# Moving the subtraction and clamp of five of eight decay tiles into the slots of the conv units, in place in the broadcast tiles

## What is computed

```
A_cum  = cumsum(dt * A)                       # per head, over a chunk
L      = exp(A_cum[l] - A_cum[s])  for l >= s, else 0
Y_diag = einsum('bzlhn,bzshn,bhzls,bzshp->bzlhp', Cc, Bc, L, xch)
...
xc     = silu(depthwise_conv(hBC))            # 4 taps over the tokens
g      = y * silu(gate);  out = normed(g) @ out_proj_w.T
```

## Time and profile before

| | |
|---|---|
| time, median of 3 runs | 2678.79 us (2675.01 to 2682.47) |
| the profiled execution | 2688.24 us, its span 2686.5 us |
| granted TensorE clock, mean | 0.980 |
| busy over the span | TensorE 93%, VectorE 69%, ScalarE 58%, GpSimd 53% |
| the mixer | from 1066.4 us to 2573.9 us of the span |

### The profile page before, as it was taken

How to read it: one execution, slowest core, us unless ns; L and a number is a source line. 1 busy time by engine, 2 the same in 40 slices (tenths; PEclk the granted TensorE clock), 3 DMA queues, 4 the chain that set the end, 5 groups by cost and what they waited for, 6 DMA issues and landing times.

```text
span 2686.5 us, 60496 instructions
## 1 busy us (share of the span) xinstructions
PE 2508.8 (93%) x19326; PEld 2014.3 (75%) x19326; DVE 1859.6 (69%) x2707; ACT 1565.2 (58%) x3539; POOL 1425.6 (53%) x1396
## 2 busy tenths in 40 slices
PE   5999999999999678899999999999999999999989
PEld 4778788788788467677777777777777777777777
DVE  4776666766767677677777677687677777786864
ACT  3544535535445254766865775786677658757821
POOL 1654655656546000556656565575666566565720
PEclk8999999999999789999999999999999999999999
DMA  4022220220230024323222222222232132222111
GB/s 111 26 81 42 50 78 29 65 74 23 75 70 8 19 91 145 109 64 108 95 67 89 96 84 68 96 100 68 80 107 85 64 104 99 76 78 94 56 40 48
DMA packets 93549, 198.84 MB, mean 74 GB/s; under 512 B 11248, under 2 KB 19440, under 8 KB 93296
## 3 DMA queue, kind: packets, MB, share of 16 engines
q1 hardware_dynamic: 93296, 195.64, 23.3%
HBM read 184.46 MB, written 11.14 MB: 73 GB/s over the span
## 4 chain that ended last, share of the span: by engine, by line
PE 28%; DVE 12%; issue 10%; ACT 10%; POOL 5%; ACTq 1%; DVEq 1%; DMA 0%; POOLq 0%; SPq 0%
PE proj L214 6%; PE proj L216 6%; PE proj L215 6%; DVE mx_acc L1170 3%; ACT decay L1484 3%; ACT mx_decay L1484 2%; PE core_y L1360 2%; DVE slab_lo L197 2%; POOL mx_hd L1629 1%; POOL mx_gate L1633 1%; ACT mx_HS L1470 1%; PE core_o L1366 1%; DVE bc_acc L1170 1%; ACT mx_decay L1488 1%; DVE mx_hd L1547 1%
## 5 line engine op out<-in xcount | busy, mean ns | idle before, releaser
L197 DVE TENSOR_TENSOR slab_lo<-slab_raw,slab_hi 128x512 fp32r<-128x512 f32 (+2 forms) x272 | 262.8, 978 | 177.2 <-ACT slab_hi L188 149.7
L214 PE MATMUL proj<-slab_hi,XTL 128*128 128x512 f32 x816 | 348.6, 427 | 5.1 <-DVE mx_gate L1576 2.7
L214 PE MATMUL proj<-XTH,slab_lo 128*128 128x512 f32 x736 | 301.2, 409 | 35.0 <-DVE at_ropeB L874 14.1
L216 PE MATMUL proj<-slab_hi,XTH 128*128 128x512 f32 x816 | 320.1, 392 | 0.0
L215 PE MATMUL proj<-slab_lo,XTH 128*128 128x512 f32 x816 | 319.0, 391 | 0.0
L215 PE MATMUL proj<-XTL,slab_hi 128*128 128x512 f32 x736 | 292.5, 397 | 0.0
L216 PE MATMUL proj<-XTH,slab_hi 128*128 128x512 f32 x736 | 292.4, 397 | 0.0
L1616 POOL TENSOR_TENSOR mx_th<-mx_th,mx_acc 128x512 f32<-128x512 f32 x48 | 62.2, 1296 | 370.3 <-ACT mx_th L1515 370.3
L214 PE MATMUL proj<-slab_hi,mx_otl 128*128 128x512 f32 x576 | 241.7, 420 | 2.1 <-DVE mx_otl L263 2.1
L1633 POOL TENSOR_TENSOR mx_gate<-mx_gate,mx_hd 128x512 f32<-128x512 f32 x128 | 170.2, 1330 | 133.1 <-DVE mx_hd L1547 122.1
L216 PE MATMUL proj<-slab_hi,mx_oth 128*128 128x512 f32 x576 | 227.6, 395 | 0.0
(11 more groups left out here) (353 smaller groups left out, 6770.0 us busy)
## 6 DMA issues: line engine op xcount, KB each, us to landing
mx_g_all<-sums SPq DMA_DIRECT2D x128, 512.0 KB, 3.7
at_g_all<-sums SPq DMA_DIRECT2D x64, 256.0 KB, 8.0
slab_raw<-in_w_gate SPq DMA_DIRECT2D x64, 256.0 KB, 2.9
slab_raw<-in_w_out SPq DMA_DIRECT2D x64, 256.0 KB, 2.9
slab_raw<-in_w_x SPq DMA_DIRECT2D x60, 256.0 KB, 4.4
slab_raw<-in_w_q SPq DMA_DIRECT2D x32, 256.0 KB, 2.9
slab_raw<-in_w_g SPq DMA_DIRECT2D x32, 256.0 KB, 8.4
slab_raw<-in_w_o SPq DMA_DIRECT2D x32, 256.0 KB, 2.9
```

Source lines behind the costliest of these rows:

```text
L197: op = nc.vector.tensor_tensor(K.SL[par][:, c, 0:width], K.RAW[c][:, 0:width], hi, ALU.subtract)
L214: nc.tensor.matmul(to[:, 0:bh.shape[-1]], al, bh, start=(c == 0), stop=False)
L216: mm = nc.tensor.matmul(to[:, 0:bh.shape[-1]], ah, bh, start=False, stop=(c == KC - 1))
```

## The change

The Relu of a tile is written back into its `GB` tile instead of into the bank, and the Exp reads from there. So the Relu no longer needs the bank, and those of tiles 1 to 4 are put behind the tanh in the conv slots 0 to 7 (one half tile, four Relu, per slot), those of tile 0 into slots 21 and 22 of the half before. Tiles 5 to 7 keep their slots, but both half tiles' Relu now stand ahead of both Exp. A fifth `GB` tile is added; tiles 0 to 2 share theirs with 5 to 7, and the row loads wait for other readers. A plain `nop` (`alone`) is issued ahead of each row load. No instruction that computes is added or removed.

```diff
-        GB = [sb(f"g_all{i}", [P, HH1, P]) for i in range(4)]
+        GB = [sb(f"g_all{i}", [P, HH1, P]) for i in range(5)]
+        ROW_OF = [0, 1, 2, 3, 4, 0, 1, 2]
+        EARLY = {sl: (sl // 2 + 1, sl % 2) for sl in range(8)}
+        NEXT = {OFF + 13: (0, 0), OFF + 14: (0, 1)}
...
-            def row_load(q, t):
-                sp.wait_ge(S["mx_e"], HEAD + 16 * q + 2 * t - 6)
+            def row_load(q, t, read):
+                i = ROW_OF[t]
+                src = sums[t:t + 1, ds(HH1 * P * q, HH1 * P)].broadcast_to([P, HH1 * P])
+                sp.wait_ge(S["mx_e"], HEAD + 16 * q + read)
+                alone(sp)
...
-            for t in range(4):
-                row_load(0, t)
+            for t in range(5):
+                row_load(0, t, 0)
...
-                    for t in range(4, NT):
-                        row_load(q, t)
+                    for t in range(5, NT):
+                        row_load(q, t, 2 * (t - 5) + 2)
...
-                        for t in range(4):
-                            row_load(q + 1, t)
+                        for t, reader in ((3, 3), (4, 4), (0, 5), (1, 6), (2, 7)):
+                            row_load(q + 1, t, 2 * reader + 2 - 16)
...
+            def differences(q, t, k):
+                i = ROW_OF[t]
+                act.wait_ge(S[f"mx_row{i}"], HEAD + (32 * q + 16 * (1 + (t >= 5)) if i < 3 else 16 * (q + 1)))
+                alone(act)
+                for h in range(4 * k, 4 * k + 4):
+                    rl = nc.scalar.activation(GB[i][:, h, :], GB[i][:, h, :], ACT.Relu,
+                                              bias=upto[:, t, ds(HH1 * q + h, 1)], scale=-1.0)
+                rl.then_inc(S["mx_rl"], 1)
...
                     if r in SCORE1:
                         t = SCORE1.index(r)
-                        act.wait_ge(S[f"mx_row{t % 4}"], HEAD + 32 * q + 16 * (t // 4 + 1))
+                        if t >= 5:
+                            for k in range(2):
+                                differences(q, t, k)
                         for k in range(2):
                             act.wait_ge(S["mx_m"], HEAD + 16 * q + 2 * t + k - 1)
...
-                            alone(act)
-                            for h in range(4):
-                                rl = nc.scalar.activation(PD[k][:, h * P:(h + 1) * P], GB[t % 4][:, 4 * k + h, :], ACT.Relu,
-                                                          bias=upto[:, t, ds(HH1 * q + 4 * k + h, 1)], scale=-1.0)
-                            rl.then_inc(S["mx_rl"], 1)
                             act.wait_ge(S["mx_rl"], HEAD + 16 * q + 2 * t + k + 1)
-                            nc.scalar.activation(PD[k][:, :], PD[k][:, :], ACT.Exp, scale=-1.0).then_inc(S["mx_e"], 1)
+                            nc.scalar.activation(PD[k][:, :], GB[ROW_OF[t]][:, 4 * k:4 * k + 4, :].rearrange("p h n -> p (h n)"), ACT.Exp,
+                                                 scale=-1.0).then_inc(S["mx_e"], 1)
...
+                    if sl in EARLY:
+                        differences(q, *EARLY[sl])
+                    if sl in NEXT and not (last and s == 1):
+                        differences(q + 1, *NEXT[sl])
+            for k in range(2):
+                differences(0, 0, k)
```

More of the change, by code:

```diff
@@ L165 @@
     + ["bc_ld", "bc_a", "bc_tap", "bc_cm", "bc_st0", "bc_st1", "bc_st2", "bc_st3"]
-    + ["mx_ld", "mx_bc", "mx_row0", "mx_row1", "mx_row2", "mx_row3", "mx_a", "mx_tap", "mx_th", "mx_cm", "mx_hsT", "mx_pt", "mx_hs",
+    + ["mx_ld", "mx_bc", "mx_row0", "mx_row1", "mx_row2", "mx_row3", "mx_row4", "mx_a", "mx_tap", "mx_th", "mx_cm", "mx_hsT", "mx_pt", "mx_hs",
        "mx_pof", "mx_cb", "mx_bt", "mx_e", "mx_m", "mx_xc", "mx_hd", "mx_xd", "mx_y", "mx_yb",
@@ L1310, in slab @@
                     load_chunk(K, sp, N + 3 * q + j, c, whole(w[ds(q + (j == 3), 1), :, c, :]))
-            def row_load(q, t):
-                sp.wait_ge(S["mx_e"], HEAD + 16 * q + 2 * t - 6)
-                sp.dma_start(GB[t % 4][:, :, :].rearrange("p h n -> p (h n)"), sums[t:t + 1, ds(HH1 * P * q, HH1 * P)]
-                             .broadcast_to([P, HH1 * P])).then_inc(S[f"mx_row{t % 4}"], 16)
+            def row_load(q, t, read):
[3 more added lines that the diff above has]
+                alone(sp)
+                sp.dma_start(GB[i][:, :, :].rearrange("p h n -> p (h n)"), src).then_inc(S[f"mx_row{i}"], 16)
             sp.dma_start(tri[:, :], d["tri"]).then_inc(S["mx_ld"], 16)
```

## The result

The changed kernel takes 2652.11 us (median of 4 runs, 2650.94 to 2656.66); the kernel before, on the same chip, 2680.63 (4 runs, 2675.01 to 2687.98). The ratio is 0.9895 with a 95% interval of 0.9867 to 0.9923: 28.5 us less (21 to 36), where 15.5 were forecast (2663.3, range 2650 to 2680). The profiled execution took 2650.94, its span 2649.2.

A forecast was written before the change was run, and what follows sets the result against it. TensorE bounds the kernel, finally waiting for ScalarE's overfull queue in slots 8 to 14. Terms -13.0 - 5.0 + 0.7 + 1.8 = -15.5 us, from a median of 2678.79 to 2663.3, range 2650 to 2680.

The forecast's parts named there:

- Step 1: Relu out of slots 8 to 14: waits for gated tile, `HS` copies and slot 10 gate go, 29.6 us gross.
- Step 2: Relu into even halves' conv slots: no cost to TensorE, each half keeps a 1.62 us gain, 13.0 for eight.
- Step 3: Relu into odd halves' conv slots: 0.3 late at slot 7, 1.0 at slot 10; net -0.62 per half, -5.0 us.
- Step 4: Tiles 5 to 7, both groups ahead of both Exp: late waits (`mx_xch`, `mx_hd`) stay, zero effect.
- Step 5: Tile 0's Relu in slots 21 and 22: delays the last tile's high part in even halves, 0.7 us lost.
- Step 6: SyncE's fifth row load ahead of the first weights: 1.8 us lost once at the start; other loads no later.
- ScalarE becomes the bound of the conv slots: Rival, 10%: at 1.5 instead of 1.18 us per group, conv slots delay each silu; +10 us, 2689.
- The gain is eaten by the next in line: Rival, 17%: VectorE or GpSimd holds the gated tile, slot 14's wait only halves; -4 us in total, 2675.
- The conv slots hide everything: Rival, 15%: ScalarE's waits for TensorE in most conv slots absorb the moved Relu; 2651 to 2655 us.

## Why the forecast had the direction and the mechanism right and the size too small

*Step 1* (the Relu out of slots 8 to 14) held. All three waits are gone, and with them the 29.6 us that they cost by the forecast's count. It was a little more: from the turn in slot 12 to that in slot 14 an even half went from 9.4 to 8.1 us, 1.3 and not the 1.13 that I had counted.

*Step 2* (even halves at no cost) held: no new wait, the middle is 1.9 shorter, against 1.62 forecast. In sum that is 15 for 13.0. A whole even half between two turns of the loop takes 91.2 to 92.4 us in both profiles, under the 92.6 forecast.

*Step 3* (odd halves) had the chain right and its result too small. Its links, ScalarE and GpSimd in conv slots 4 and 7 of an odd half and TensorE at slots 7 and 10, of the changed kernel:

```profile
1546.76 0.77 ACT L1160 ACTIVATE mx_acc<-mx_decay,conv_b,conv_w 128x512 f32<-128x512 f32 x1
1547.42 0.62 ACT L1527 ACTIVATE mx_to<-mx_hd 128x512 f32<-128x512 f32 x1
1547.94 1.28 ACT L1457 ACTIVATE mx_g_all<-mx_g_all,upto_sum 128x128 f32<-128x128 f32 x4
...
1555.99 0.78 ACT L1160 ACTIVATE mx_hd<-core_y,conv_b,conv_w 128x512 f32<-128x512 f32 x1
```

```profile
1548.19 1.30 POOL L1634 TENSOR_TENSOR mx_to<-mx_to,mx_hd 128x512 f32<-128x512 f32 x1 [0.63 <-ACT mx_to L1527]
1549.64 1.30 POOL L1637 TENSOR_TENSOR mx_hd<-mx_to,mx_hd 128x512 f32<-128x512 f32 x1
```

```profile
1551.17 0.60 PE L1395 MATMUL mx_normed<-ident,mx_hd 128*128 128x128 f32 x4
...
1563.00 1.10 PE L1365 MATMUL core_y<-mx_xch,mx_m 128*32 128x64 f32 x64 [1.66 <-DVE mx_m L1578]
1564.11 0.50 PE L214 MATMUL proj<-slab_hi,XTL 128*128 128x512 f32 x1
```

Measured from the start of the half (2106.05 before, 1530.64 now), the conv start of slot 4 is 1.17 later (forecast 1.18), the tanh of unit 3 0.93 later (0.97), the silu's start 0.67 later (0.72). The silu itself took 2.75 from its start to its end and not 3.17, since its first step took 1.30 where the earlier trace rows have 1.73; it ended at 1550.94, 0.23 ahead of the turn, and the 0.3 of wait at slot 7 did not come. The last conv start is 1.3 later (1.56), the unit of slot 10 33.47 into the half and not 32.48: 0.99 later, forecast 1.0. The wait there shows as 1.66, not as about 1, since in before other waits (0.43 for the gate among them) stood in that place.

The step that failed is the last one, "1.0 - 0.49 - 1.13 = -0.62". It took the waits of the late slots as fixed. GpSimd's copy `mx_xch` and what stands behind it, in the changed kernel:

```profile
1604.72 1.04 POOL L1672 TENSOR_TENSOR mx_xch<-mx_HS,dt 128x512 f32<-128x512 f32 x1
```

```profile
1605.86 0.83 PE L1365 MATMUL core_y<-mx_xch,mx_m 128*32 128x64 f32 x45 [0.75 <-POOL mx_xch L1672]
```

In the ten microseconds and more ahead of it GpSimd works with gaps of 0.23 us at most, in both kernels, so its start follows that of its queue. Before that GpSimd waits for VectorE's `mx_to`, and VectorE starts this stretch in step with TensorE: its `mx_ACC` waits for a unit of TensorE and starts 56.02 into the half before and 55.14 now. So at this point VectorE is 0.88 ahead, just as TensorE is (0.82 at slot 14, 0.87 at slot 16). What follows, VectorE's next step and GpSimd's release, first in the kernel before, then in the changed one:

```profile
2162.92 1.11 DVE L1584 SCALAR_TENSOR_TENSOR X<-mx_ACC,mx_r,X 128x512 f32<-128x512 f32 x1 [0.16 <-DVE mx_ACC L1581]
...
2165.97 1.29 POOL L1629 TENSOR_TENSOR mx_hd<-mx_hd,mx_to 128x512 f32<-128x512 f32 x1 [1.04 <-DVE mx_to L1553]
```

```profile
1586.64 0.75 DVE L1602 SCALAR_TENSOR_TENSOR X<-mx_ACC,mx_r,X 128x512 f32<-128x512 f32 x1 [0.17 <-DVE mx_ACC L1599]
...
1589.34 1.29 POOL L1647 TENSOR_TENSOR mx_hd<-mx_hd,mx_to 128x512 f32<-128x512 f32 x1 [1.04 <-DVE mx_to L1571]
```

The same VectorE step takes 0.36 less, so GpSimd is released 1.24 earlier (59.93 and 58.69), and its own instructions from there to `mx_xch` take 0.2 less (15.57 and 15.38). So `mx_xch` starts 74.08 into the half instead of 75.50, 1.42 earlier, and the wait of 1.30 shrinks to 0.75. In slot 22 0.12 come back (`mx_otl`). That makes -1.3 per odd half instead of -0.62: 10 to 11 us for eight in place of 5.0. Of the 0.7 more, 0.2 are the waits of slots 12 and 14, which paid back 0.47 and 1.35, and 0.55 are the late wait. The 0.55 are no lateness handed on: they are instructions of two engines that took less time, in the first of these steps in all seven odd halves of both profiles of each kernel, in the second in six of seven. The seventh is the first odd half, where one copy `mx_xch` of that queue took 1.55 and not 1.05, and there the late wait is 1.03. So the durations make the wait; what makes the durations stays open. The kernel with fewer groups in slots 4 to 7 bears it out: its VectorE step takes 0.93 and its GpSimd queue 15.58, and though TensorE is 1.65 earlier at slot 14 than in the changed kernel, `mx_xch` is only 1.25 earlier and its wait is 1.1 again.

*Step 4* (tiles 5 to 7 at zero) held: the old order measures the same. Its "late waits stay" held for `mx_hd` (3.6 and 3.6), not for `mx_xch`, by the way just told and not by the order.

*Step 5* (0.7 for the high part in slot 22) held nearly: from the last turn of an even half to the next half 6.02 became 6.17, 1.2 us for eight.

*Step 6* (1.8 for the fifth load) held for the loads: alone they put 1.6 on the first silu wait. In the changed kernel it is 0.9, for TensorE could turn the first silu 3.58 and not 4.11 after its tanh started: GpSimd's second step took 1.26 instead of 1.79, for a reason that I did not follow.

*Not in the sum* was the turn of the loop. The heads fell from 12.9 to 12.3 on average (two profiles each), 3 us for six; but the stretch behind slot 22 in odd halves, on the other side of the same turn, grew from 7.1 to 7.3 at the six turns and from 6.57 to 6.89 at the last, 1.7 us. As single ones of both differ by about 1 us between executions, I hold a gain of the turn for possible and not for shown. There is also a cost that I had not seen as one. Slots 4 and 5 of the even half that starts at 1636.26 in the kernel before, where TensorE lost 2.0 to the silu, in windows (TensorE's clock is the third number from the right):

```profile
1645.50:1649.50 4.00, 2.15 (x11) 1.50 (x10) 3.57 (x6) 2.80 (x5) 3.40 (x3) 1.00 0.08 23
1649.50:1653.50 4.00, 4.00 (x18) 3.60 (x17) 3.58 (x6) 1.63 (x3) 3.71 (x4) 0.57 0.12 43
```

After the wait the granted clock fell: 0.57 is the mean over 4 us, and in single microseconds from 1650 to 1653 it is 0.50, the lower of the two levels (1.2 of 2.4 GHz). The middle of that half took 76.7 instead of 75.1. That happened in two of seven even halves in each profile of the kernel before (3.2 us), in none of those of the changed one.

The sum of the parts is then, from the middle: 15 (even) + 11 (odd) + 3 (heads) + 3 (clock) - 1 (behind slot 22, even) - 2 (behind slot 22, odd) = 29; the two pairs of profiles give 33.4 and 27.2 from the first turn of a silu to the last gated turn. The runs say 28.5.

Of the rivals, "ScalarE becomes the bound of the conv slots" named the right place and a price far too high: 0.3 more per group cost 9 to 10 us, not 25. "The gain is eaten by the next in line" did not come true; after the gate's wait none took its place behind it. "The conv slots hide everything" is the time that came (2652), but not its way: odd halves do lose 1.3 us to the new groups, and other waits paid for it. The range held the result 2 us from its lower end, and partly by luck: its lower bound, 2651, was reckoned for delays that stay hidden, and what made up the difference, the late wait and the clock, stands in none of its terms. With the groups placed elsewhere 2644 was to be had.

## What to carry to other kernels

Moving work within an in-order queue is worth what the queue was late by at the places where the next engine waits, and it costs at the new place only what its gaps don't hold; both can be read from the start of the same instruction, counted from the start of the loop's turn, in two profiles. Follow it link by link to the end of the turn, and past the first wait that vanishes: here a late wait shrank by 0.55 us a half although no instruction of VectorE or GpSimd, which make it, was moved, since some of them took less time beside the new order. An estimate that holds the durations fixed misses that. And fill a gap only as far as it goes: half of the groups in odd conv slots were free, the other half cost 1.3 us a half, and slots two or three ahead of their Exp took them at no cost that shows.

## What of the hardware was not expected

- The same ScalarE instruction costs 391 ns into SBUF and 362 to 370 into PSUM (Relu, 128x128), and 602 against 582 by its source (Exp, 128x512); 6 us of 2683 by the runs, 7 by the middles, when all 16 groups of a half are changed in a full queue.
- The same VectorE step (`X`, 128x512) takes 0.75 to 0.77 us at one place of the odd half in the changed kernel and 1.05 to 1.12 at the same place in the kernel before, and 0.93 to 0.97 with fewer groups in slots 4 to 7, in all seven odd halves looked at of each profile. A slot later, where it runs beside GpSimd's `mx_xch`, it takes 0.86 to 0.93 and the copy 1.49 or 1.50 in all seven halves of the kernel before; in the changed one it takes 1.64 to 1.66 and the copy 1.03 to 1.05 in six halves, 0.75 and 1.55 in one. One of the two is always the longer, so they seem to slow each other, but no run here isolates that.
- In the two profiles of the kernel before, 9 silu waits at the turn of the loop lost 1.95 to 2.41 us; four of them were followed by a middle of 76.7 to 76.8 instead of 75.1, each with three to four us at a granted clock of 0.50. Of the three at 1.06 to 1.22, and of the twelve in the changed kernel at 0.75 to 2.1, none was. Nor does the length of the wait alone decide: behind the wait of slot 10, 1.71 to 1.72 each time, the clock fell in three of seven odd halves with two short Relu more, and in none with one, where the wait was 1.75 to 1.78.
